# A two-layer graph kernel: another order of loads, casts and roundings in the first rows, and staging work spread over the steady rows

## The reference, cut to what matters

```python
deg = jnp.clip(adj.sum(axis=1), 1.0)
dis = deg ** (-0.5)
diffusion = (dis[:, None] * adj * dis[None, :]) @ x - x
norms = jnp.maximum(jnp.linalg.norm(x, axis=-1), 1e-8)
sim = x @ x.T / (norms[:, None] * norms[None, :])
attn = jax.nn.softmax(beta * sim * adj, axis=1)
x = layernorm(x + diffusion + sigmoid(alpha) * (attn @ x - x))
x = layernorm(x + relu(adj @ (x @ weights)))
```

## Time and profile before

| | us |
|---|---|
| median of 3 runs | 694.9 (694.83 to 694.93) |
| the profiled execution | 695.17 |
| its span, first to last instruction | 693.4 |
| PE busy | 660.7 (95%) |
| DVE busy | 569.1 (82%) |
| ACT busy | 430.4 (62%) |
| POOL busy | 248.7 (36%) |
| mean granted TensorE clock | 0.984 of full speed |

### The profile page before, as it was taken

The page is one execution under the profiler, slowest core; times in us unless marked ns, Lnnn a source line. Parts: engine busy times, 40 slices in busy tenths (PEclk is TensorE's granted clock), DMA queues, the critical chain, the costliest instruction groups (busy, mean ns, idle before and its releaser), DMA issues.

```text
span 693.4 us, 18265 instructions
## 1 busy us (share of the span) xinstructions
PE 660.7 (95%) x5651; PEld 524.8 (76%) x5651; DVE 569.1 (82%) x1684; ACT 430.4 (62%) x873; POOL 248.7 (36%) x225
## 2 busy tenths in 40 slices
PE   6868999999999999999999998699999999999997
PEld 6536777777777777777777776598888888888886
DVE  4857999999999999999999999876767676666664
ACT  5867999989898898999999997202222223111111
POOL 2699344644546455464464555600000000000000
PEclk8999999999999999999999999899999999999999
DMA  7687799999999999999999993400000000000000
GB/s 250 186 237 182 189 243 249 260 248 257 243 257 261 242 267 235 258 250 252 244 254 257 255 237 68 61 5 1 0 0 0 0 0 1 17 15 30 15 15 30
DMA packets 154532, 105.25 MB, mean 152 GB/s; under 512 B 135696, under 2 KB 136208, under 8 KB 154512
## 3 DMA queue, kind: packets, MB, share of 16 engines
q1 hardware_dynamic: 154512, 105.01, 59.5%
HBM read 69.34 MB, written 2.10 MB: 103 GB/s over the span
## 4 chain that ended last, share of the span: by engine, by line
PE 87%; DVE 5%; POOL 4%; issue 1%; ACT 1%; DMA 1%; SPq 0%; DVEq 0%; POOLq 0%; ACTq 0%
PE ps_e L1015 30%; PE ps_s L926 21%; PE ps_e L958 8%; PE ps_e L937 7%; PE ps_acc L958 7%; PE ps_e L961 4%; PE ps_acc L961 4%; PE ps_s L975 1%; PE ps_e L975 1%; DVE stage L703 1%; DMA x_keep<-in_x 1%; DVE scores L632 1%; POOL x_parts L344 1%; PE ps_at L910 1%; POOL u L359 1%
## 5 line engine op out<-in xcount | busy, mean ns | idle before, releaser
L926 PE MATMUL ps_s<-xn_parts,xn_signed 128*128 128x512 f16 x756 | 205.4, 382 | 10.3 <-POOL xn_signed L303 7.5
L632 DVE CUSTOM_DVE_ANT_1 scores<-ps_s,adj_bytes 128x512 f32<-128x512 f32 x252 | 171.5, 681 | 27.4 <-issue 14.1
L445 ACT ACTIVATE scores<-scores,col 128x1024 f32<-128x1024 f32 x128 | 157.4, 1232 | 9.5 <-DVE col L643 9.4
L326 POOL TENSOR_SCALAR e_parts<-scores 128x1024 f16<-128x1024 f32 x64 | 84.0, 1312 | 166.4 <-ACT scores L445 113.6
L413 ACT ACTIVATE adj_bytes<-land 128x1024 uint8<-128x1024 f32 x128 | 133.6, 1048 | 0.0
L1015 PE MATMUL ps_e<-x_parts,stage 128*128 128x256 f16 x1024 | 113.0, 273 | 0.0
L1015 PEld LDWEIGHTS ps_e<-x_parts,stage 128*128 128x128 fp8e4 x1024 | 100.2, 98 | 11.5
L452 ACT ACTIVATE eT_parts<-ps_e 128x512 f16<-128x512 f32 x128 | 75.8, 592 | 53.1 <-PE ps_e L937 52.5
L1015 PE MATMUL ps_e<-y_parts,stage 128*128 128x256 f16 x896 | 105.4, 273 | 0.2
L926 PEld LDWEIGHTS ps_s<-xn_parts,xn_signed 128*128 128x128 f16 x756 | 70.0, 98 | 46.8 <-POOL xn_signed L303 7.9
L653 DVE SCALAR_TENSOR_TENSOR e_parts<-scores,e_parts 128x1024 f16<-128x1024 f32 x64 | 96.0, 1499 | 0.1
(11 more groups left out here) (130 smaller groups left out, 1003.2 us busy)
## 6 DMA issues: line engine op xcount, KB each, us to landing
land<-in_adj SPq DMA_DIRECT2D x128, 512.0 KB, 4.5
x_keep<-in_x SPq DMA_DIRECT2D x4, 512.0 KB, 6.9
out<-u SPq DMA_DIRECT2D x7, 256.0 KB, 2.0
eTx<-e_parts SPq DMA_TRANSPOSE x64, 4.5
out<-u SPq DMA_DIRECT2D x1, 192.0 KB, 1.9
eT_parts<-in_L_gnn_weights SPq DMA_DIRECT2D x1, 64.0 KB, 7.9
scores<-in_L_gnn_weights SPq DMA_DIRECT2D x1, 64.0 KB, 1.8
out<-u SPq DMA_DIRECT2D x1, 64.0 KB, 1.6
```

The lines of the kernel that those rows point to most:

```text
L326: nc.gpsimd.tensor_scalar(e_parts[:, n, 0, :], scores[:, q, (n + 2) * CH:(n + 3) * CH], E_SCALE, 1.0, ALU.mult, ALU.mult).wait_op(sign_don ...
L445: nc.scalar.activation(piece, piece, ACT.Exp, bias=neg_max[q], scale=abs_beta, accum_out=csum[:, q, i:i + 1]).then_inc(exp_done, 1)
L632: nc.vector.tensor_tensor_reduce(scores[:, q, o:o + BANK].rearrange("p (k q) -> p k q", k=K), score_bank(h, r == 0 if start else False).re ...
L926: ins = nc.tensor.matmul(score_bank(h, start), xn_signed[:, q, part, :], xn_parts[:, other, o:o + BANK], start=(part == 0 and other == 0), ...
```

## The change

1. **Loads.** SP issues the four quarters of x first, then alpha and beta. DVE's three instructions on the sign of beta move behind `rnorm(3)`.
2. **ACT and DVE in the start.** `norm_root(1)` moves ahead of `squares(2)`, and `norms2(3)` ahead of `rnorm(2)`. The eight evictions of `xn_parts` are no longer interleaved with the casts of row 0: one cast stands behind the fourth, three behind the eighth. The casts of row 1 are placed otherwise among the first exps.
3. **x parts.** ACT rounds quarters 0 and 2 (`x_high`), after the scales are known and ahead of the first exps. POOL scales both, then makes both low parts, then does `pack(0, 0)`, `ex_high`, `sign_block(2, 0)`, `ex_high`, and only then quarters 1 and 3.
4. **Staging.** The twelve pieces of blocks 0, 1 and 2 leave rows 30 and 31. In the steady rows DVE issues one piece in every second row, behind `row_max`, up to row 25. So that the number of the piece can be a constant, the loop is `Fori(0, 3)` over eight rows; rows 26 to 29 stand behind it in full. In the list of DVE's instructions the loop has 467 entries, before 123.
5. **y.** ACT rounds y (`y_high`) in place of POOL; each `y_low` moves behind an `ex_low` or one step later.

```diff
-            for q in range(1, C):
-                sp.dma_start(x_b[:, 2 * q:2 * q + 2, :], x_v[:, 2 * q:2 * q + 2, :]).then_inc(x_loaded[q], 16)
...
+            x_scale(0)
+            x_scale(2)
+            x_low(0, 0)
+            x_low(1, 2)
+            pack(0, 0, first=True)
+            ex_high(0, 0, 0, first=True)
+            sign_block(2, 0)
+            ex_high(0, 0, 1, first=True)
+            for n, q in ((2, 1), (3, 3)):
+                pool.wait_ge(x_hi, n)
+                x_high(q)
+                x_scale(q)
+                x_low(n, q)
...
-                pool.wait_ge(y_done, q + 1)
-                nc.gpsimd.tensor_scalar(y_parts[:, q * TC:(q + 1) * TC, 0, :], y_q, 1.0, 1.0,
-                                        ALU.mult, ALU.mult).then_inc(y_hi, 1)
...
+            def x_high(q):
+                nc.scalar.activation(x_parts[:, q * TC:(q + 1) * TC, 0:D], x_keep[:, q * TC:(q + 1) * TC, :], ACT.Copy,
+                                     scale=x_up).then_inc(x_hi, 1)
...
+            turned_high(0)
+            turned_high(1)
+            norm_root(3)
+            turned_high(2)
+            turned_high(3)
             cast(0, 0, 0, first=True)
...
+            for g in range(4, H):
+                turned_high(g)
+            for i in range(1, C):
+                cast(0, 0, i, first=True)
...
+            cast(1, 1, 0, first=True)
             act.wait_ge(scales_done, 1)
-            cast(1, 1, 1, first=True)
+            x_high(0)
+            x_high(2)
...
+            y_high(0)
             for b in range(TB):
                 e_high(R - 1, b)
                 if b == 0:
                     nc.scalar.activation(table_loads[2], eps_c, ACT.Sqrt)
+                if b < C - 1:
+                    y_high(b + 1)
...
+                    if h == 3 and spread:
+                        stage_block(spread[0], spread[0], (spread[1],))
...
-            with dve.Fori(2, R - 3, 2) as r:
-                row(r, 0)
-                row(r + 1, 1)
+            with dve.Fori(0, G - 1) as n:
+                for i in range(C):
+                    r = n * (2 * C) + (2 * i + 2)
+                    row(r, 0)
+                    row(r + 1, 1, spread=(n, i))
+            for r in range(2 * C * (G - 1) + 2, R - 2):
+                row(r, r % 2)
...
-                if h in (0, 2, 4):
+                if h in (1, 3, 5):
                     y_low(h // 2 + 1)
-                if h == 0:
-                    stage_block(1, 1, (2, 3))
```

More of the change, by code:

```diff
@@ L336, in _, with x_scale, x_low @@
             pool.wait_ge(scales_done, 1)
[L337 to L341, removed]
+            def x_scale(q):
+                nc.gpsimd.tensor_scalar(u[:, q * TC:(q + 1) * TC, :], x_keep[:, q * TC:(q + 1) * TC, :], x_up, 1.0,
+                                        ALU.mult, ALU.mult).then_inc(x_scaled, 1)
+            def x_high(q):
+                nc.gpsimd.tensor_scalar(x_parts[:, q * TC:(q + 1) * TC, 0:D], x_keep[:, q * TC:(q + 1) * TC, :], x_up, 1.0,
+                                        ALU.mult, ALU.mult).then_inc(x_hi, 1)
+            def x_low(n, q):
                 pool.wait_ge(x_scaled, n + 1)
                 pool.wait_ge(x_hi, n + 1)
[L344 to L350, removed]
+                nc.gpsimd.tensor_tensor(x_parts[:, q * TC:(q + 1) * TC, D:2 * D], u[:, q * TC:(q + 1) * TC, :],
+                                        x_parts[:, q * TC:(q + 1) * TC, 0:D], ALU.subtract).then_inc(x_lo, 1)
+            x_scale(0)
[11 more added lines that the diff above has]
+                x_low(n, q)
             pack(1, 1, first=True)
@@ L465, in _ @@
             exps(0, 0, 2)
+            exps(0, 0, 3)
+            cast(1, 1, 1, first=True)
+            exps(0, 0, 0)
+            exps(0, 0, 1)
             cast(1, 1, 2, first=True)
-            exps(0, 0, 3)
-            exps(0, 0, 0)
             cast(1, 1, 3, first=True)
-            exps(0, 0, 1)
             row(0, 0, start=True)
@@ L475, in _, with y_high @@
                 row(r + 1, 1)
+            def y_high(q):
+                act.wait_ge(y_done, q + 1)
+                nc.scalar.activation(y_parts[:, q * TC:(q + 1) * TC, 0, :], x_keep[:, q * TC:(q + 1) * TC, :],
+                                     ACT.Copy).then_inc(y_hi, 1)
             e_high(R - 2, 0)
@@ L724, in y_low, with row @@
                                         y_parts[:, q * TC:(q + 1) * TC, 0, :], ALU.subtract).then_inc(y_lo, 1)
-            def row(r, q, start=False, second=False, last_two=False):
+            def row(r, q, start=False, second=False, last_two=False, spread=None):
                 for h in range(H):
@@ L737, in row @@
                         mask(r + 2, q, h - C)
-                    if last_two and h in (4, 5):
-                        stage_block(0, 0, ((0, 1), (2, 3))[h % 2])
                     if h % 2 == 0:
@@ L751, in row @@
                         store_adj(r)
-                    if last_two and h == 6:
-                        y_low(0)
                     if h == 7:
@@ L756, in row @@
                     if last_two and h == 7:
-                        stage_block(1, 1, (0, 1))
+                        y_low(0)
                     if h in (3, 4, 6):
@@ L781, in _ @@
                     store_adj(R - 1)
-                    stage_block(2, 2)
                 if h in (3, 4, 6):
```

28 lines of the change are left out of this document (14 added, 14 removed).

## The result

The changed kernel took 692.2 us (median of 5; 690.7 to 693.8), the kernel before beside it 694.9: a ratio of 0.996 (0.9941 to 0.9979). Measured once more later beside 29 executions of before, it gave 1.0011 (0.9993 to 1.0029). So the change is worth between nothing and 2.7 us, where 8.3 were forecast, and 692.2 lies above the range of 682.5 to 690.5. The profiled execution of the changed kernel, 693.76, is the slowest of its five.

What follows compares the result with a forecast made beforehand. The prediction took PE to bound the steady rows, with gains only in the start and handover: 3.7 (start) + 6.6 (handover) - 0 (staging) - 2.0 (longer loop) = 8.3 us, from 694.9 to 686.6 us, range 682.5 to 690.5.

Steps and rivals of the forecast that it cites:

- What bounds the kernel: Steady rows: PE is the limit, busy 10.00 of 10 us; gains only at 40 to 70 and 430 to 450 us.
- Loads and start: Start: x's second quarter lands near 5.6 us, 3.1 sooner; with the new x parts, ex_high(1,1,0) comes 3.7 us earlier.
- (c): Start: rival that x's quarters still come at 8.7 us, leaving 0.6 us of the start's gain: 689.7 us, chance 0.11.
- Staging in the steady rows: Rows 3 to 25: twelve pieces of about 0.3 us each fill DVE's waits for PE; cost 0, at most 3.6 us.
- The longer loop: DVE's eight-row loop: instruction fetches at two back edges cost PE 1.0 us each, 2.0 us lost, bounds 0 and 7.2.
- (b): DVE's loop edges: rival that the fetch costs its full upper price, 7.2 us: 691.8 us, chance 0.08.
- (a): DVE's loop: rival that the long loop costs nothing, as the short one: 684.6 us, chance 0.20.
- The handover: Handover to the adjacency sums: without staging pieces and POOL's y roundings, PE reaches the piece of 457.77 near 451.2: 6.6 us gained.
- e_low 0.6, ex_low 1.5, y_low(1) 1.3: Handover, after y_low(0) at 437.9: these three steps, in us, give 441.3, before PE's second piece ends at 442.2.
- (d): Handover: rival that it stays bound by a lower clock and DVE and POOL slowing each other, 3.5 us gained: 689.7, chance 0.11.
- The sum: Whole kernel: 3.7 + 6.6 - 0 - 2.0 = 8.3 us gained, from 694.9 to 686.6 us.
- (e): Whole kernel: rival that the changed kernel is slower than before; its forecast time isn't in the text; chance 0.03.

Runs made afterwards that it cites:

- the written-out kernel: The changed kernel with VectorE's rows 2 to 29 written out one after the other, no loop, the twelve staging pieces where they stood: 686.1 us, ratio 0.9876 to before.

## Why the prediction was wrong

**What bounds the kernel: right.** PE at 10.00 in the steady rows, gains only in the start and the handover, and everything else can only lose. It did.

**Loads and start: right, a little large.** The second squares came at 5.50 (5.6 forecast), the first x_low at 26.50 (27.85), ex_high(1,1,0) at 49.36 (49.8), the sign block of row 3 at 57.99 (58.4). The lead is 4.1 us in this trace and 3.5 in the mean of the traces (3.7 forecast), 2.7 by the comparison. That the small loads hold x is shown by the run that put them back (second squares at 10.09 against 5.39 us); so (c) is out. PE's wait for the sign block of row 3 wasn't its only one left (2.86 us, up from 2.05): it also stood 2.25 us for the exps at 32.16 and 2.23 for a DMA transpose at 42.15.

**Staging in the steady rows: right.** Cost 0, and still 0 when doubled.

**The longer loop: the step that failed.** That both edges would pay was assumed, and no row of before shows it; the gaps of 3.49 and 3.51 us do. Right too were their places, the packets and PE's reserve (3.49 - 2.32 = 1.2 us, 1.0 forecast). The price was not. I took a fetch of 3.2 us, between 1.8 and 4.5, and took 1.22 us of ex_low and 1.0 of PE off it. The idle time of VectorE begins where ex_low ends, and is still 3.5 us. The branch has no row, but if the fetch begins no later than ex_low, as I assumed, it takes at least 4.7 us, above my upper price of 4.5, and up to 5.4 + 1.2 in a four-row loop. And PE's loss isn't its wait: waits of 2.32 and 2.27 us became slips of 4.2 and 2.8. Behind the first stood the lower clock (0.50 from 173 to 175 us), but that isn't the whole reason: when the changed kernel was measured again the clock stayed at 1.00 behind both edges, and waits of 2.41 and 1.21 at the first became a slip of 5.1, one of 2.25 at the second 3.0; in before with eight rows it stayed behind waits of 2.9, slips 3.3. Instead of 2.0 us the two edges cost 5.8 by the first comparison and 9.4 by the second. I had placed the fetch in the middle of two transfers that were no instruction fetches, 1.8 and 4.5 us, instead of at the loaded end. Case (b), at 691.8, lies next to the 692.2, in part by luck: its edges cost 7.2 where this comparison has 5.8, and its other gains are 10.3 where the runs have 8.6.

Two counts in the arguments on the loop were off. The 467 instructions leave out those that only wait or set registers; with them the body has 554. And PE's loop of two rows, named for (a) as the longer one, has 462 in a trip of the trace: it is shorter than VectorE's new body.

**The handover: right in kind, 0.7 us short by the comparison (5.9 against 6.6), 1.6 by the trace (5.0).** y_low(0) came about when forecast (440.5 less the 3.4 us of entering late is 437.1, 437.9 forecast), from a y_high that came later than forecast and a y_low of 1.23 us instead of 2.3. What failed is "e_low 0.6, ex_low 1.5, y_low(1) 1.3". VectorE and POOL of the written-out kernel:

```profile
433.51 2.32 DVE L683 SCALAR_TENSOR_TENSOR e_parts<-scores,e_parts 128x1024 f16<-128x1024 f32 x1
435.75 2.91 DVE L753 TENSOR_TENSOR y_parts<-x_keep,y_parts 128x1024 f16<-128x1024 f32 x1
...
431.87 5.72 POOL L391 TENSOR_TENSOR x_keep<-x_keep,norm_r 128x1024 f32<-128x1024 f32 x2
```

POOL, freed of its roundings, now scales its last two y quarters just beside them (the y_low that follows, at 439.19 us with POOL idle, takes 1.21 in place of 2.91), and PE waits 1.42 us there, 1.92 in the changed kernel. Its wait for the exps also grew from 1.81 to 2.75 us, since PE comes to it earlier. I had put ACT's rounding down as a part of the gain; it is worth nothing beside the staging. Of (d) one sign is there in the written-out kernel: the granted clock is 0.83 over 430 to 440 us, and eight matmuls at 433.14 take 1.53 us. Its 3.5 us are out all the same, against 5.9.

**The sum.** Without the loop, start and handover are worth 8.6 us (0.9876), of 10.3 forecast. The rest of the miss is the loop. Case (a), that the long loop is free, is out in every run without the hint. Case (e), slower than before, is out too (0.996 and 1.0011): in the profile of the changed kernel the straight code within a trip has no gap.

## What to carry to other kernels

Price a loop body by its back edges before anything that it makes possible: here, on VectorE, 144 instructions were free and 278 cost 5.7 us per edge (nothing between was tried). If a constant needs a longer body, write the rows out, put the work into a few written-out rows behind the short loop (685.7 us here), or use the back edge's hint (695.0 in place of 729.3 with four rows). I would put a wait that has no row in the profile at the loaded end of its nearest rows: here it was at least 4.7 us by my estimate, beside 4.5 for the row under load and 1.8 for the quiet one. And a PE that stood for over 2 us cost more than it stood here (2.3 to 2.9 us of waiting became 2.8 to 4.2 of slip).

## What was not expected of the hardware

A hint removes the wait altogether where the body is 278 instructions long (42 packets become 12), but with the body of 554 the packets stay (29 with it and without), and one wait of 4.05 us stands behind the loop. The price of an edge varies within one execution: six edges of the same loop left VectorE idle for 3.98 to 5.44 us. Whether it also varies from one execution to the next isn't shown: the repeated changed kernel's twelve lie within 5.3 us, but so nearly do the 29 of before beside it, which has no such edge (4.9). And two broadcasts of 0.5 KB between the loads of x held ACT's second squares back by 4.7 us, from 5.39 to 10.09, in the run that put them back (to 8.73 in before).
